# Zeroing a DRAM buffer from the SyncE queue, copied out of DRAM, one head pair earlier

## The chip, the core and the metric

One core of a Trainium2 chip runs the whole kernel. The metric is device time in microseconds (us), from start to end of one execution. Lower is better.

## What is computed

A graph transformer block over N = 1250 nodes with D = 768 features and 20000 edges: a layer norm, then a graph convolution plus polynomial attention over 12 heads, then a switch layer with 8 experts of 195 slots each. Cut to what matters here:

```
xn = _layernorm(x)
A = q @ k.T                              # per head, 1250 x 1250
numerator = 1.0 + A + 0.5 * A * A
attn = numerator / numerator.sum(-1)
mix = (attn @ v) @ w_proj + b_proj
x = x + gnn(xn, edges) + mix
# switch layer on xf = _layernorm(x)
keep = rank < capacity                   # capacity 195 slots for each of 8 experts
buf = zeros(E + 1, capacity, D).at[dest_e, dest_c].set(xf)
o = gelu(buf[:E] @ w1 + b1) @ w2 + b2
out = where(keep, o[routes, dest_c], xf) * prob_max
```

`buf` is what this case is about. A slot that no node is routed to must read as zero, so its DRAM copy, `rows`, is zeroed before the nodes are scattered into it.

## The kernel before

The engines run their own instruction streams and meet at semaphores. Five blocks follow each other.

1. Load, layer norm, transposes and values. VectorE also starts to turn edges into cell indices of `counts`, the 1250 x 1250 table of edge counts in DRAM. GpSimd adds them into that table in indirect transfers, two columns of 128 edges at a time; each pair of columns waits until the pair before has landed.
2. Attention, one head pair after another, j = 0 to 5 (`turn(j, last)` on each engine). A pair is 30 steps: TensorE makes the scores of a step, ScalarE squares them (`Pf`), ScalarE or VectorE rounds them (`Ph`), VectorE makes the rest (`Pl`), TensorE multiplies by `vsb`, the values. Step i's scores need step i-2's squares, since two score buffers alternate. Among the steps of pair j the projections of pair j+1 are made, so that its first step can start at once. GpSimd's edge additions run beside pairs 0 to 5; the last 20 columns are released by VectorE in step 24 of pair 4.
3. `pairs_over`: all engines wait for the end of the pairs. SyncE then also waits for the last edge addition and loads `counts`.
4. Graph convolution, projection, second layer norm, routing.
5. GpSimd scatters the nodes into `rows`; experts; gather and output.

SyncE (SP) issues nearly all transfers, in the order of its code. In pair j it loads the values (`load_v`) and weights (`load_w`), copies each half of the keys to the other 64 partitions (`second_half`: KHB and KLB for the second head, KHA and KLA for the next pair's first head), stores and reloads the inverse denominators (`store_inverse`, `load_inverse`: `invd`, `rden`) and stores the result (`odram`). TensorE's step 0 of the next pair waits for the KHA and KLA copies (`k_twice`), and VectorE's `finish` at step 30 waits for `rden`.

`rows` has 1560 slot rows and 1250 rows for nodes past the capacity, 768 floats each: 2810 x 768 x 4 B = 8.63 MB. ScalarE issues its zeroing in step 4 of the last pair (`CLEAR_AT = 4`), in three transfers out of `strip`, a zeroed SBUF tile of 384 columns. The scatter of block 5 and `pairs_over` wait for it (`r_zero`).

Of the kernel before, what the change touches and what calls it, by code (L numbers as in the profile page):

```python
# [25 lines left out]
F32 = mybir.dt.float32  # L26
F32R = mybir.dt.float32r
BF16 = mybir.dt.bfloat16
# [6 lines left out]
P = 128  # L35
N, D = 1250, 768
T, NT = 125, 10
KT = D // P
HALF = D // 2
# [12 lines left out]
EP = (ET - EARLY) // 5  # L52
# [3 lines left out]
WINDOW = 2  # L56
# [7 lines left out]
CAP = int(1.25 * N / E)  # L64
SLOTS = E * CAP
CAPP = CAP + 1
CTILES = [(0, 105), (105, 90)]
CROWS = 105
STEPS = 30
# [16 lines left out]
def at(start, size):  # L86
    return bass.ds(start, size)
# [3 lines left out]
MOVED = 16 * len(PARTS)  # L91


def move(eng, to, of, landed):

    for p0, n in PARTS:
        eng.dma_start(to[p0:p0 + n], of[p0:p0 + n]).then_inc(landed, 16)  # L97


def build(nc, x, src, dst, gnn_w, gnn_b, w_qkv, b_qkv, w_proj, b_proj, sw, sb_, w1, b1, w2, b2, out,  # L100
          counts, keyd, vdram, odram, rows, x1d, invd):
    ctx = ExitStack()
    with ctx:
        def sem(name):
# [5 lines left out]
        def region(specs):  # L110

            with ExitStack() as inner:
                return [inner.enter_context(nc.sbuf_tensor(*s)) for s in specs]
# [4 lines left out]
        def right(stack, specs):  # L118
# [34 lines left out]
        r_zero = sem("r_zero")  # L153
# [5 lines left out]
        padded = sem("padded")  # L159
        consts, carrier = sem("consts"), sem("carrier")  # L160
# [20 lines left out]

        (K32, kt2, KHA, KLA, MA, gs, Q32, OUN, R32, rden, vsb, tmpo, Pf, Ph, Pl, k1, inv, invr, KHB, KLB, MB, OHL, eqp, kcur, ccur, strip) = region([
            ("K32", [P, N], F32), ("kt2", [P, NT, 2, P], F32R),
            ("KHA", [P, N], F32R), ("KLA", [P, N], F32R), ("MA", [P, N], F32R), ("gs", [P, 3, P], F32),
            ("Q32", [P, N], F32), ("OUN", [P, N], F32), ("R32", [P, N], F32), ("rden", [P, N], F32),
# [1 line left out]
            ("Pf", [T, RING, 2, CW], F32), ("Ph", [T, RING, 2, CW], F32R), ("Pl", [T, RING, 2, CW], F32R),  # L189
            ("k1", [P, 4], F32), ("inv", [T, 2, NT], F32), ("invr", [2 * NT, T], F32),  # L190
            ("KHB", [P, N], F32R), ("KLB", [P, N], F32R), ("MB", [P, N], F32R),
            ("OHL", [P, 2, N], F32R), ("eqp", [P, 2, WINDOW * P], BF16), ("kcur", [P, EP], F32), ("ccur", [P, EP], F32),
            ("strip", [P, HALF], F32)])
        KH, KL, MQ = (KHA, KHB), (KLA, KLB), (MA, MB)
        kbp = kt2[:].rearrange("p t l f -> p (t l) f")
        keys_in, eq_over = sem("keys_in"), sem("eq_over")
# [83 lines left out]
        @block.sync  # L280
        def _(sp):
            for i in range(NT):
                move(sp, xn[:, i, :], x[i * T:(i + 1) * T, :], x_in[i // 2])
                if i == 1:
                    for wc in range(3):
                        sp.dma_start(w_staging(wc), w_parts[0][0][2 * wc * P:2 * (wc + 1) * P, :].rearrange(
                            "(k p) n -> p k n", p=P)).then_inc(w_early[wc], 16)
            sp.wait_ge(keys, 2)
            sp.dma_start(keyd[0:P, :], keyA[:]).then_inc(key_out, 16)
            sp.dma_start(keyd[P:, :], keyB[:]).then_inc(key_out, 16)  # L290
            for s_ in (1, 0):
                sp.dma_start(ws[:, s_], w_qkv[:, s_ * D:s_ * D + P].rearrange("(k p) n -> p k n", p=P)
                             ).then_inc(wqk_in[s_], 16)
            sp.wait_ge(key_out, 32)

            def load_keys(half, slot, c, n):

                sp.dma_start(kb[:, half, slot:slot + n, :], keyd[c:c + n, :].unsqueeze(0).broadcast_to([P, n, P])
                             ).then_inc(kb_in[half], 16)

            load_keys(0, 0, 0, EC)
            sp.wait_ge(w_lo, 3)
            load_keys(1, 0, EC, EC)
            for i in range(NT):
                sp.wait_ge(v_lo, 2 * i + 2)
                move(sp, vdram[:, i, :].rearrange("(j p) f -> p j f", p=T),
                     VS[:, i % 2].bitcast(F32).rearrange("p (j a) l f -> p j (a l f)", a=2), v_store[i % 2])
                if i == FIRST_EDGES + 1:
                    sp.wait_ge(eq_done, 2)
                    load_keys(0, 0, 2 * EC, EC)  # L310
                if i == FIRST_EDGES + 3:
                    sp.wait_ge(eq_done, 4)
                    load_keys(1, 0, 3 * EC, EARLY - 3 * EC)
                    load_keys(1, EARLY - 3 * EC, LONE, 1)
# [319 lines left out]
        def values_over(eng):  # L634

            eng.wait_ge(v_store[0], MOVED * NT // 2)
            eng.wait_ge(v_store[1], MOVED * NT // 2)
            eng.wait_ge(v_mm, 2 * NT)
            eng.wait_ge(idx_ready, EU)
            eng.wait_ge(scattered, CLEARED)  # L640

        PAIR_KEYS_AT = 5
        COMPARE_AT = (6, 7, 7, 8, 10, 10, 11, 12, 13, 14, 15, 15, 16, 17, 17, 18, 20, 20, 21, 22)
        PAIR_TARGETS_AT = 23
        CLEAR_AT = 4

        @block.sync
        def _(sp):
# [16 lines left out]
            def second_half(a, n):  # L665

                own, other = slice(a * HD, (a + 1) * HD), slice((1 - a) * HD, (2 - a) * HD)
                for done, part in ((k_hi[a], KH[a]), (k_lo[a], KL[a])):
                    sp.wait_ge(done, n)
                    sp.dma_start(part[other, :].bitcast(F32), part[own, :].bitcast(F32)).then_inc(k_twice, 16)  # L670
# [14 lines left out]
            def load_inverse(j):  # L685

                sp.wait_ge(inv_out, 16 * j + 16)
                for a in range(2):
                    sp.dma_start(rden[a * HD:(a + 1) * HD, :],
                                 invd[at(j * 2 * NT + a * NT, NT), :].rearrange("i t -> (i t)").unsqueeze(0).broadcast_to([HD, N])  # L690
                                 ).then_inc(rden_in, 16)

            load_pair_keys(0)

            def turn(j, last, keyed):
                sp.wait_ge(oacc_done, 6 * j + FREE)
                load_v(j, 1)
                if not last:
                    sp.wait_ge(wqk_lo, 2 * j + 3)
                    load_w(j + 2, 1)  # L700
                second_half(1, 3 * j + 3)
                if not last:
                    sp.wait_ge(wqk_lo, 2 * j + 4)
                    sp.sem_inc(carrier, 1)
                    load_w(j + 2, 0)
                    store_inverse(j)
                    sp.wait_ge(pv_done, j * STEPS + STEPS // 2)
                    load_v(j + 1, 0)
                    load_inverse(j)
                    second_half(0, 3 * j + 6)  # L710
                    if keyed:
                        load_pair_keys(j + 1)
                else:
                    store_inverse(j)
                    load_inverse(j)
                    sp.wait_ge(g_mm, PAIRS)
                    for wc in (3, 4, 5):
                        load_w3(sp, wc)
                sp.wait_ge(o_fin, 3 * j + 3)
                for l in range(2):  # L720
                    sp.dma_start(odram[at(j * P, P), :, l, :],
                                 OHL[:, l, :].bitcast(F32).rearrange("p (i t) -> p i t", t=T)).then_inc(o_store, 16)
                if not last:
                    sp.wait_ge(o_store, 32 * j + 32)
                    sp.sem_inc(ohl_free, 1)
# [7 lines left out]
        def _(act):  # L733
# [48 lines left out]
            def turn(j, last):  # L782
# [22 lines left out]
                for i in range(END):  # L805
# [8 lines left out]
                        round_weights(i - 1)  # L814
                    if i == OWN_READ_AT:
                        read_kq(j, 5)
                    if last and i == CLEAR_AT:
                        act.wait_ge(padded, 2)
                        act.dma_start(rows[0:SLOTS, :].rearrange("(p s) (h d) -> p (s h) d", p=120, h=2),
                                      strip[0:120, :].unsqueeze(1).broadcast_to([120, 26, HALF])).then_inc(r_zero, 16)  # L820
                        move(act, rows[SLOTS:, :].rearrange("(p s) (h d) -> p (s h) d", p=T, h=2),
                             strip[0:T, :].unsqueeze(1).broadcast_to([T, 2 * NT, HALF]), r_zero)
                    if i in SECOND_AT:
                        hi_part(1, j, SECOND_AT.index(i))
                    if i in LATE_AT:
# [35 lines left out]
        def _(dve):  # L861
# [42 lines left out]
            pair_bias(0)  # L904
            dve.sem_inc(oacc_done, FREE)
            values_over(dve)
            dve.memset(strip[:], 0.0).then_inc(padded, 1)
            before = Chain(dve, pair_order)
            split_w(1, 1)
            for n in range(3):  # L910
# [272 lines left out]
        def pairs_over(eng):  # L1183

            eng.wait_ge(wqk_lo, 2 * PAIRS + 1)
            eng.wait_ge(wqk_in[0], 16 * (PAIRS + 1))
            eng.wait_ge(pv_done, PAIRS * STEPS)
            eng.wait_ge(tmp_done, 6 * PAIRS)
            eng.wait_ge(r_zero, 16 + MOVED)
            eng.wait_ge(o_fin, 3 * PAIRS)  # L1190

        @block.sync
# [307 lines left out]
        @block.gpsimd  # L1500
        def _(pool):
            pool.wait_ge(slot_done, 1)
            pool.wait_ge(xf_done, NT)
            pool.wait_ge(r_zero, 16 + MOVED)
            for i in range(NT):
                pool.indirect_dma_start(out=rows, out_offset=bass.IndirectOffsetOnAxis(ap=slots[:, i:i + 1], axis=0),  # L1506
                                        in_=XF[:, i, :], in_offset=None).then_inc(sent, 16)
# [289 lines left out]
```

## Time and profile before

| what | value |
|---|---|
| median of 3 runs | 1167.61 us (1166.87 to 1172.84) |
| profiled execution, its own time | 1170.61 us |
| its span, first to last instruction | 1168.9 us |
| mean granted TensorE clock | 0.915 |
| busy in the span: TensorE, VectorE, ScalarE, GpSimd | 936.1, 733.1, 459.5, 308.2 us |
| DMA queue 10 (ScalarE's), bytes | 8.80 MB |
| DMA queue 1 (SyncE's), bytes | 128.82 MB |

The profile counts only compute as busy: an engine whose sequencer is held while it issues a transfer shows up as idle, and the issue itself stands in the timeline as ACTq or SPq. All times of rows are from the start of the span, so the profiled execution's own time is 1.7 us more than the span.

### The profile page before, as it was taken

What the parts mean: (1) busy time and instruction counts of PE and PEld (TensorE: products, weight loads), DVE (VectorE), ACT (ScalarE), POOL (GpSimd) and SP (SyncE); (2) the same over time, 40 slices, a digit from 0 to 9 for tenths busy, and PEclk for the clock granted to TensorE, in tenths of its full rate; (3) what the DMA queues carried; (4) which work ended last, traced back from release to release, by engine and by line L of the source; (5) the groups of instructions that cost most, each with busy time, mean ns of one, the idle gap of its engine ahead of it and who ended that gap; (6) DMA issues with size and microseconds to landing.
All of it is one profiled execution on the core that took longest, in us unless ns stands there. A gap on an engine that the chain in (4) does not pass through costs nothing.

```text
span 1168.9 us, 15230 instructions
## 1 busy us (share of the span) xinstructions
PE 936.1 (80%) x5250; PEld 890.3 (76%) x5250; DVE 733.1 (63%) x1397; ACT 459.5 (39%) x678; POOL 308.2 (26%) x201
## 2 busy tenths in 40 slices
PE   3896789989899899899526679699999974199970
PEld 3896788888788789788426579699999974199970
DVE  5776278889878888888425825654454526066633
ACT  2311366666657657566325602111010111166620
POOL 2035465526456445563312000000000002200004
PEclk9898899999999999999859979999999975599995
DMA  9966523543643543732893085462535312879987
GB/s 270 319 167 148 103 23 59 91 77 58 111 71 55 100 70 63 142 51 36 169 210 82 27 155 129 113 159 78 149 88 135 93 57 72 206 232 273 281 221 264
DMA packets 147431, 152.23 MB, mean 130 GB/s; under 512 B 72211, under 2 KB 125546, under 8 KB 146364
## 3 DMA queue, kind: packets, MB, share of 16 engines
q1 hardware_dynamic: 112889, 128.82, 42.4%
q0 software_dynamic: 28432, 14.05, 9.3%
q10 hardware_dynamic: 6067, 8.80, 3.2%
q8 instruction: 26, 0.43, 0.2%
q14 instruction: 17, 0.14, 0.0%
HBM read 97.16 MB, written 46.78 MB: 123 GB/s over the span
## 4 chain that ended last, share of the span: by engine, by line
PE 56%; DVE 15%; issue 9%; ACT 8%; DMA 6%; ACTq 2%; POOL 2%; SPq 1%; DVEq 0%; POOLq 0%
PE ps L1765 13%; PE ps L1767 12%; PE ps L1766 12%; PE ps L1150 6%; PE ps L1134 3%; PE ps L1135 3%; ACT Ph L789 3%; ACT Pf L811 2%; DVE Pl L1008 2%; ACTq L97 2%; DMA rows<-oE 1%; DVE Ph L1006 1%; POOL rows L1506 1%; PE ps L1399 1%; DMA rows<-XF,slots 1%
## 5 line engine op out<-in xcount | busy, mean ns | idle before, releaser
L361 POOL DMA_INDIRECT counts<-countc,idxu x157 | 273.4, 1742 | 321.8 <-DMA counts<-countc,idxu 238.5
L1008 DVE SCALAR_TENSOR_TENSOR Pl<-Pf,Ph 125x832 fp32r<-125x832 f32 (+1 forms) x180 | 184.4, 1026 | 74.1 <-ACT Ph L789 70.3
L811 ACT ACTIVATE Pf<-ps 125x832 f32<-125x832 f32 (+1 forms) x180 | 155.8, 867 | 181.4 <-PE ps L1135 137.8
L1150 PE MATMUL ps<-Ph,vsb 125*128 125x416 f32 (+1 forms) x360 | 132.3, 368 | 9.6 <-DVE Pl L1008 9.5
L1150 PE MATMUL ps<-Pl,vsb 125*128 125x416 f32 (+1 forms) x360 | 128.2, 356 | 0.0
L1506 POOL DMA_INDIRECT rows<-XF,slots x10 | 14.8, 1482 | 361.9 <-DVE slots L1621 359.1
L1134 PE MATMUL ps<-MA,KHA 128*125 128x416 f32 (+1 forms) x180 | 71.1, 395 | 44.2 <-ACT Pf L811 33.8
L1765 PE MATMUL ps<-XH,wqkH 128*128 128x416 f32 (+1 forms) x216 | 81.4, 377 | 19.9 <-DVE R L926 10.2
L1765 PE MATMUL ps<-wH,XH 128*125 128x384 f32 x240 | 85.1, 355 | 9.8 <-DVE OHL L953 5.8
L1150 PEld LDWEIGHTS ps<-Ph,vsb 125*128 125x128 f32 x360 | 69.3, 192 | 19.7 <-DVE Pl L1008 9.3
L1766 PE MATMUL ps<-wL,XH 128*125 128x384 f32 x240 | 83.8, 349 | 0.0
L1767 PE MATMUL ps<-wH,XL 128*125 128x384 f32 x240 | 83.6, 348 | 0.0
L1006 DVE TENSOR_SCALAR Ph<-Pf 125x832 fp32r<-125x832 f32 (+1 forms) x90 | 55.7, 619 | 40.2 <-ACT Pf L811 33.9
L789 ACT ACTIVATE Ph<-Pf 125x832 fp32r<-125x832 f32 (+1 forms) x90 | 79.9, 895 | 0.7
L1766 PE MATMUL ps<-XL,wqkH 128*128 128x416 f32 (+1 forms) x216 | 77.7, 360 | 0.0
L1767 PE MATMUL ps<-XH,wqkL 128*128 128x416 f32 (+1 forms) x216 | 77.7, 360 | 0.0
L1765 PE MATMUL ps<-HH,CH 125*125 125x384 f32 x200 | 69.4, 347 | 7.0 <-DVE CL L1322 7.0
L1134 PE MATMUL ps<-MB,KHB 128*125 128x416 f32 (+1 forms) x180 | 65.7, 365 | 8.5 <-ACT Pf L811 8.5
L1134 PEld LDWEIGHTS ps<-MA,KHA 128*125 128x125 f32 x180 | 34.4, 191 | 49.6 <-ACT Pf L811 40.2
L1150 PEld LDWEIGHTS ps<-Pl,vsb 125*128 125x128 f32 x360 | 69.5, 193 | 0.9
L1767 PE MATMUL ps<-HH,CL 125*125 125x384 f32 x200 | 68.4, 342 | 0.0
L1766 PE MATMUL ps<-HL,CH 125*125 125x384 f32 x200 | 68.4, 342 | 0.0
(236 smaller groups left out, 2176.5 us busy)
## 6 DMA issues: line engine op xcount, KB each, us to landing
Cs<-counts SPq DMA_DIRECT2D x20, 546.9 KB
w1s<-L_ffn_w SPq DMA_DIRECT2D x8, 1152.0 KB, 8.9
w2s<-L_ffn_w SPq DMA_DIRECT2D x8, 1152.0 KB, 6.6
odram<-OHL SPq DMA_DIRECT2D x12, 625.0 KB, 8.5
oS<-odram SPq DMA_DIRECT2D x10, 750.0 KB, 4.8
vdram<-VS SPq DMA_DIRECT2D x10, 672.0 KB
vsb<-vdram SPq DMA_DIRECT2D x12, 560.0 KB
kt<-keyd SPq DMA_DIRECT2D x5, 1280.0 KB, 6.1
```

The costliest lines, as they stand in the source:

```text
L361: pool.indirect_dma_start(out=counts, out_offset=bass.IndirectOffsetOnAxis(ap=idxu[:, c:c + 1], axis=0), in_=countc[:, c:c + 1], in_offset ...
L789: act.activation(Ph[:, i % RING, :, 0:w], Pf[:, i % RING, :, 0:w], ACT.Identity, bias=1.0).then_inc(p_hiA, 1)
L811: act.activation(Pf[:, i % RING, :, 0:w], ps[0:T, 2 * (i % 2):2 * (i % 2) + 2, 0:w], ACT.Square, bias=1.0).then_inc(sq_done, 1)
L1006: dve.tensor_scalar(h, f, 1.0, None, ALU.add).then_inc(p_hiD, 1)
L1008: dve.scalar_tensor_tensor(out=p, in0=f, scalar=1.0, in1=h.bitcast(F32), op0=ALU.add, op1=ALU.subtract).then_inc(p_lo, 1)
L1134: pe.matmul(out_, KH[a][:, kt * T:(kt + 1) * T], q, start=True, stop=False)
L1135: ins = pe.matmul(out_, KL[a][:, kt * T:(kt + 1) * T], q, start=False, stop=True)
L1150: ins = pe.matmul(ps[:, 4 + s % 2, 0:w], vsb[:, 2 * kp + t, a, :], part[:, m % RING, t, 0:w], start=(kp == 0 and t == 0 and part is Ph), s ...
L1506: pool.indirect_dma_start(out=rows, out_offset=bass.IndirectOffsetOnAxis(ap=slots[:, i:i + 1], axis=0), in_=XF[:, i, :], in_offset=None).t ...
L1765: pe.matmul(out, lh, rh, start=(k == 0), stop=False)
L1766: pe.matmul(out, lh, rl, start=False, stop=False)
L1767: ins = pe.matmul(out, ll, rh, start=False, stop=(k == tiles - 1))
```

## The change

The three transfers of ScalarE, the tile `strip` and its memset go. A DRAM tensor `blank` of 1686 floats (6744 B) is written once, early, by a small transfer of SyncE out of the tile `zeros`. In pair 4 (the second-to-last) SyncE then zeroes `rows` in two DRAM to DRAM transfers, each of 16 x 40 runs that all read `blank`: `clear(0)` behind the KLB copy, `clear(1)` between `load_inverse` and the KHA copy. `pairs_over` no longer waits for them; the scatter of block 5 does. Each half is 16 x 40 x 6744 B = 4.32 MB.

```diff
@@ block 1, SyncE
             sp.dma_start(keyd[P:, :], keyB[:]).then_inc(key_out, 16)
+            sp.wait_ge(consts, 1)
+            sp.dma_start(blank.rearrange("(p d) -> p d", p=6), zeros[0:6, 0:BLANK // 6]).then_inc(r_zero, 16)
@@ block 2, SyncE
+            def clear(half):
+
+                n = (SLOTS + N) * D // (32 * BLANK)
+                sp.dma_start(rows.rearrange("r d -> (r d)").rearrange("(a b c) -> a b c", a=16, c=BLANK)[:, half * n:(half + 1) * n],
+                             blank.unsqueeze(0).unsqueeze(0).broadcast_to([16, n, BLANK])).then_inc(r_zero, 16)
+
                 second_half(1, 3 * j + 3)
+                if not last and not keyed:
+                    sp.wait_ge(r_zero, 16)
+                    clear(0)
...
                     load_inverse(j)
+                    if not keyed:
+                        clear(1)
                     second_half(0, 3 * j + 6)
@@ block 2, ScalarE
-                    if last and i == CLEAR_AT:
-                        act.wait_ge(padded, 2)
-                        act.dma_start(rows[0:SLOTS, :].rearrange("(p s) (h d) -> p (s h) d", p=120, h=2),
-                                      strip[0:120, :].unsqueeze(1).broadcast_to([120, 26, HALF])).then_inc(r_zero, 16)
-                        move(act, rows[SLOTS:, :].rearrange("(p s) (h d) -> p (s h) d", p=T, h=2),
-                             strip[0:T, :].unsqueeze(1).broadcast_to([T, 2 * NT, HALF]), r_zero)
@@ block 2, VectorE
-            dve.memset(strip[:], 0.0).then_inc(padded, 1)
@@ pairs_over
-            eng.wait_ge(r_zero, 16 + MOVED)
@@ block 5, GpSimd
-            pool.wait_ge(r_zero, 16 + MOVED)
+            pool.wait_ge(r_zero, 48)
```

ScalarE's queue in the last pair, from step 3's square on. Before:

```order
L747 ACTIVATE Q<-ps,pbias 128x416 [waits qk_mm]
L756 ACTIVATE KHB<-K 64x416 [waits kq_full]
L811 ACTIVATE Pf<-ps 125x836 [waits p_lo,sc_done]
L789 ACTIVATE Ph<-Pf 125x836 [waits pv_done,sq_done]
L819 DMA rows<-strip 3120x1x384 [waits padded]
L97 DMA rows<-strip 2240x1x384
L97 DMA rows<-strip 260x1x384
L811 ACTIVATE Pf<-ps 125x2x416 [waits p_lo,sc_done]
L758 ACTIVATE MA<-Q 64x416 [waits kq_full]
```

Of the change:

```order
L760 ACTIVATE Q<-ps,pbias 128x416 [waits qk_mm]
L769 ACTIVATE KHB<-K 64x416 [waits kq_full]
L824 ACTIVATE Pf<-ps 125x836 [waits p_lo,sc_done]
L802 ACTIVATE Ph<-Pf 125x836 [waits pv_done,sq_done]
L824 ACTIVATE Pf<-ps 125x2x416 [waits p_lo,sc_done]
L771 ACTIVATE MA<-Q 64x416 [waits kq_full]
```

The three transfers between step 4's rounding and step 5's square are gone; the rest stands as it was.

SyncE's queue in pair 4, behind the KLB copy. Before:

```order
L670 DMA KLB<-KLB 64x1250 [waits k_lo1]
L657 DMA ws<-L_mix_w_qkv 128x6x128 [waits wqk_lo]
L683 DMA invd<-invr 20x125 [waits inv_row]
L662 DMA vsb<-vdram 112x10x128 [waits pv_done]
L662 DMA vsb<-vdram 13x10x128
L689 DMA rden<-invd 64x1250 [waits inv_out]
L689 DMA rden<-invd 64x1250
L670 DMA KHA<-KHA 64x1250 [waits k_hi0]
L670 DMA KLA<-KLA 64x1250 [waits k_lo0]
```

Of the change:

```order
L672 DMA KLB<-KLB 64x1250 [waits k_lo1]
L700 DMA rows<-blank 16x40x1686 [waits r_zero]
L659 DMA ws<-L_mix_w_qkv 128x6x128 [waits wqk_lo]
L685 DMA invd<-invr 20x125 [waits inv_row]
L664 DMA vsb<-vdram 112x10x128 [waits pv_done]
L664 DMA vsb<-vdram 13x10x128
L691 DMA rden<-invd 64x1250 [waits inv_out]
L691 DMA rden<-invd 64x1250
L700 DMA rows<-blank 16x40x1686
L672 DMA KHA<-KHA 64x1250 [waits k_hi0]
L672 DMA KLA<-KLA 64x1250 [waits k_lo0]
```

The two halves stand in front of the weights of a later pair and in front of the KHA copy.

## Rows read from the trace of the kernel before

**Rows 1.** The page's first line.

```profile
span 1168.9 us, 15230 instructions
```

**Rows 2.** Timeline of ScalarE in the last pair: start, duration, line, idle before.

```profile
565.93 1.05 ACTq L819 DMA_DIRECT2D rows<-strip  x1
567.02 16.74 ACTq L97 DMA_DIRECT2D rows<-strip  x1
567.03 0.90 ACT L789 ACTIVATE Ph<-Pf 125x836 fp32r<-125x836 f32 x1
583.78 20.94 ACTq L97 DMA_DIRECT2D rows<-strip  x1
604.83 0.86 ACT L811 ACTIVATE Pf<-ps 125x832 f32<-125x832 f32 x1 [36.90 <-issue]
```

**Rows 3.** Timeline of TensorE, same stretch.

```profile
568.58 0.35 PE L1135 MATMUL ps<-MA,KLA 128*125 128x416 f32 x1
...
605.75 0.71 PE L1134 MATMUL ps<-MA,KHA 128*125 128x416 f32 x1 [33.80 <-ACT Pf L811]
...
610.42 0.55 PE L1150 MATMUL ps<-Pl,vsb 125*128 125x416 f32 x1
```

**Rows 4.** Timeline of VectorE, same stretch.

```profile
605.80 0.59 DVE L1006 TENSOR_SCALAR Ph<-Pf 125x832 fp32r<-125x832 f32 x1 [33.86 <-ACT Pf L811]
```

**Rows 5.** Engines' busy times by stretch; then granted clock, DMA share, GB/s.

```profile
488.00:570.00 82.00, 74.45 (x394) 69.50 (x393) 69.69 (x134) 52.37 (x76) 40.07 (x23) 1.00 0.44 69
570.00:675.00 105.00, 51.13 (x233) 44.41 (x232) 51.80 (x68) 40.82 (x52) 17.59 (x10) 0.78 0.51 121
```

**Rows 6.** Chain that ended last, from 560 us on: start, us, what.

```profile
634.04 7.02 DMA wst<-L_gnn_W
...
680.96 10.93 DMA Cs<-counts
```

**Rows 7.** DMA issues: count, KB of each, median us to landing.

```profile
kt<-keyd SPq DMA_DIRECT2D x5, 1280.0 KB, 6.1
counts<-zeros POOLq DMA_DIRECT2D x1, 5468.8 KB, 25.9
...
rows<-strip ACTq DMA_DIRECT2D x1, 4680.0 KB
...
KHA<-KHA SPq DMA_DIRECT2D x6, 312.5 KB, 3.2
```

**Rows 8.** Timeline of SyncE's queue in pair 4.

```profile
494.17 0.50 SPq L670 DMA_DIRECT2D KLB<-KLB  x1
511.64 0.38 SPq L657 DMA_DIRECT2D ws<-L_mix_w_qkv  x1
520.06 0.34 SPq L683 DMA_DIRECT2D invd<-invr  x1
...
522.12 1.16 SPq L689 DMA_DIRECT2D rden<-invd  x2
541.37 0.49 SPq L670 DMA_DIRECT2D KHA<-KHA  x1
548.31 0.48 SPq L670 DMA_DIRECT2D KLA<-KLA  x1
```

**Rows 9.** Timeline of TensorE: the first score of the last pair.

```profile
556.94 0.36 PE L1134 MATMUL ps<-MA,KHA 128*125 128x418 f32 x1
```

**Rows 10.** Timeline of GpSimd: first of a pair of columns, and the last.

```profile
538.16 1.77 POOL L361 DMA_INDIRECT counts<-countc,idxu  x1 [12.54 <-DVE idxu L979]
...
560.90 1.56 POOL L361 DMA_INDIRECT counts<-countc,idxu  x1 [2.05 <-DMA counts<-countc,idxu]
...
614.44 1.56 POOL L361 DMA_INDIRECT counts<-countc,idxu  x1 [9.09 <-DMA counts<-countc,idxu]
...
622.38 2.10 POOL L361 DMA_INDIRECT counts<-countc,idxu  x1 [0.30 <-issue]
```

**Rows 11.** Timeline of SyncE's queue behind the pairs.

```profile
679.39 4.34 SPq L97 DMA_DIRECT2D Cs<-counts  x2
```

More of the change, by code:

```diff
@@ L66 @@
 CAPP = CAP + 1
+BLANK = 1686
 CTILES = [(0, 105), (105, 90)]
@@ L100, in build @@
 def build(nc, x, src, dst, gnn_w, gnn_b, w_qkv, b_qkv, w_proj, b_proj, sw, sb_, w1, b1, w2, b2, out,
-          counts, keyd, vdram, odram, rows, x1d, invd):
+          counts, keyd, vdram, odram, rows, x1d, invd, blank):
     ctx = ExitStack()
@@ L180, in build @@
             ("VS", [T, 2, H, 2, HD], F32R), ("brow", [3 * PAIRS, P], F32)])
-        (K32, kt2, KHA, KLA, MA, gs, Q32, OUN, R32, rden, vsb, tmpo, Pf, Ph, Pl, k1, inv, invr, KHB, KLB, MB, OHL, eqp, kcur, ccur, strip) = region([
+        (K32, kt2, KHA, KLA, MA, gs, Q32, OUN, R32, rden, vsb, tmpo, Pf, Ph, Pl, k1, inv, invr, KHB, KLB, MB, OHL, eqp, kcur, ccur) = region([
             ("K32", [P, N], F32), ("kt2", [P, NT, 2, P], F32R),
@@ L191, in build @@
             ("KHB", [P, N], F32R), ("KLB", [P, N], F32R), ("MB", [P, N], F32R),
-            ("OHL", [P, 2, N], F32R), ("eqp", [P, 2, WINDOW * P], BF16), ("kcur", [P, EP], F32), ("ccur", [P, EP], F32),
-            ("strip", [P, HALF], F32)])
+            ("OHL", [P, 2, N], F32R), ("eqp", [P, 2, WINDOW * P], BF16), ("kcur", [P, EP], F32), ("ccur", [P, EP], F32)])
         KH, KL, MQ = (KHA, KHB), (KLA, KLB), (MA, MB)
@@ L640, in values_over @@
             eng.wait_ge(scattered, CLEARED)
+            eng.wait_ge(r_zero, 16)
         PAIR_KEYS_AT = 5
@@ L644, in build @@
         PAIR_TARGETS_AT = 23
-        CLEAR_AT = 4
         @block.sync
@@ L1794 @@
     invd = nc.dram_tensor("invd", (PAIRS * 2 * NT, T), F32, kind="Internal").ap()
-    build(nc, *args, result, counts, keyd, vdram, odram, rows, x1d, invd)
+    blank = nc.dram_tensor("blank", (BLANK,), F32, kind="Internal").ap()
+    build(nc, *args, result, counts, keyd, vdram, odram, rows, x1d, invd, blank)
     return _run(nc, [arrays], core_ids=[0]).results[0]["out"]
```

## The prediction

> **What bounds the kernel now.** I read the page's chain first. Its two largest entries of one kind outside TensorE's matmuls are transfers issued by ScalarE, so I went to ScalarE's timeline in the last pair. There [rows 2] its sequencer issues the three zeroing transfers. The first is accepted in 1.05 us, the second is held 16.74 us and the third 20.94 us. Behind them in the queue stands the square of step 5, which starts at 604.83 after 36.90 us without compute. Nothing else can go on: TensorE, two score buffers ahead, stands 33.80 us [rows 3], and VectorE, out of squares, 33.86 us [rows 4]. Both name ScalarE's square as what ended the idle time. By stretches [rows 5], the last pair with its end takes 105 us against 82 us for the pair before, with less work in it (TensorE 51 us busy against 74), and at a granted clock of 0.78 against 1.00. So the kernel is bound, in this one place, by ScalarE's sequencer and not by the bytes. The reader is to see that all three compute engines have the same hole.
>
> The hole hides nothing that the end needs. SyncE loads `counts` at 679.39 [rows 11]. The last edge addition is issued at 622.38 [rows 10] and needs a few us to land, so it is over about 50 us before that load.
>
> **The change, part by part.**
>
> *The three transfers leave ScalarE.* Without them, step 5's square waits only for its scores. Their last matmul starts at 568.58 and takes 0.35 us [rows 3], so the square could start at about 569.0 instead of 604.83: ScalarE comes 35.8 us earlier. VectorE's hole begins at 605.80 - 33.86 = 571.94, when that square (0.86 us, over at 569.9) would be done, so VectorE gains its whole 33.9 us. TensorE's hole begins at 605.75 - 33.80 = 571.95 and closes likewise. The least is therefore 33.8 us.
>
> On top of it comes the clock. The matmuls behind the hole take 0.55 us each until 610.42, against 0.35 before it [rows 3]. Between 605.75 and 610.77 TensorE starts some 14 matmuls about 0.35 us apart that it would start 0.19 us apart at full clock: 14 x 0.16 = 2.2 us. VectorE and ScalarE have a share in the pace there, so I count between 0 and 2.2 us of it and take 1. The term is 33.8 + 1 = 34.8, bounds 33.8 and 36.
>
> *What follows the hole* moves forward whole. The next wait for a transfer in the last pair is 7.02 us for the first piece of the next weights [rows 6], issued by SyncE after the inverse is stored. It hangs on step 17 of the same pair, so it moves with the steps and stays as long. The `counts` load moves from 679.39 to about 644.6, and its 10.93 us [rows 6] stay.
>
> *The zeroing becomes part of pair 4.* What must be priced is T, the time of one half of 4.32 MB, DRAM to DRAM. No transfer of that kind is in the trace. Nearest rows [rows 7, 2]: the first zeroing transfer, 4680 KB = 4.79 MB, was drained between 565.93 and 583.78, when the next was let in, which is 268 GB/s and gives T = 16 us. The zeroing of `counts`, 5468.8 KB = 5.60 MB, landed in 25.9 us, which is 216 GB/s and gives T = 20 us. The other side is a transfer that reads first and writes then: 20 us for the writing and, by the key broadcast (1280 KB from one small place in DRAM in 6.1 us, 215 GB/s), 20 us for the reading, so T = 40 us. That is the upper bound. I take T = 20: an engine that reads and writes at the same time is nearer to the `counts` row than to the sum, and the broadcast row shows that reading one small place over and over is not slow.
>
> The Trainium skill, page "DMA: Bandwidth & Descriptors", section "Latency and other measured facts", gives 214 GB/s for copies between HBM tensors, and about half where the rows lie a large power of two apart. Here the 16 destination rows lie 80 x 6744 B = 539,520 B apart, which is none. By that rate T would be 20.2 us, and the forecast would be the same. The same page, section "Bandwidth", puts the HBM limit of a core at about 358 GB/s; if reading and writing both draw on it, 8.63 MB for each half would make T = 24 us, and the sum would be 2 us worse by the formula below. No run here shows either yet.
>
> *Who waits for the two halves.* `clear(0)` is issued right behind KLB at 494.7 [rows 8]. It starts to move at about 498, since the value load, the weights and the two key copies are ahead of it. It ends at 498 + T = 518. The next things on the queue are weights of a pair that doesn't exist (511.64, nobody waits) and the inverse (520.06): with T under 21 both are untouched. `clear(1)` goes out at 523.3, behind the value load and the two `rden` transfers. Together they are about as many bytes as the key broadcast of 6.1 us [rows 7], so it starts to move at about 529. It ends at 529 + T = 549. Behind it stand KHA (issued 541.37) and KLA (548.31), 3.2 us each to land when alone [rows 7, 8]. Before, KLA was there at 551.6; now both land at about 552 to 553. TensorE's first score of the last pair, which waits for them, is at 556.94 [rows 9]. So at T = 20 there are some 4 us to spare and the cost is nothing. The cover is thin. Once T is over 21, `clear(0)` pushes the inverse, that pushes `clear(1)`, and both land on KHA: `clear(1)` ends at 508 + 2T, the copies land 3 us later, and the stall is 511 + 2T - 557 = **2T - 46 us**, zero at T = 23.
>
> *If SyncE is held at its issues* as ScalarE was, KHA is issued only when `clear(1)` is drained (549) and lands at 552.5, and KLA at about 556. That is still in time, by under 1 us; I add nothing.
>
> *The edge additions.* They share the 16 DMA engines. A pair of columns took (560.90 - 538.16) / 4 = 5.7 us undisturbed and (614.44 - 560.90) / 4 = 13.4 us beside the zeroing, so the zeroing cost them 4 x 7.7 = 31 us [rows 10]. Now they lose this in pair 4. The last ten pairs of columns are released at 538.16 after GpSimd idled 12.54 us, which absorbs that much. Undisturbed they would end at 538 + 10 x 5.7 + 2 = 597. If they stand still for both halves, they end at 597 + 40 - 12.5 = 625. The `counts` load is at 644.6: hidden, with 20 us to spare.
>
> *The rest.* `blank` costs SyncE one more small issue (the comparable one at 520.06 takes 0.34 us [rows 8]) in front of weights that are needed much later. The memset of `strip` stood alone, and `pairs_over` found `r_zero` long done. All of it: nothing.
>
> **The sum.** 33.8 + 1 - 0 = 34.8 us. The profiled execution's own time, 1170.6 (1.7 us over its span [rows 1]), becomes 1135.8. It was 3.0 us above the median of the three runs shown; from that median, 1167.6 - 34.8 = 1132.8. I forecast 1133.
>
> **Rivals.**
>
> 1. *The halves are hidden, as above*: 1131 to 1136. For it: T = 20 by the nearest row. Against: 3 us of T decide. Chance 0.68.
> 2. *The key copies come late.* T between 24 and 38. For it: every byte is now read from and written to DRAM, the additions take their share, and the cover is thin. Against: the rows of 16 and 20 us. At T = 26 the stall is 6 us and the time 1139; at T = 30 it is 14 and 1147; at T = 36 it is 26 and 1159. Chance 0.22, most of it (0.14) below 1150.
> 3. *Slower than before.* The same mechanism at a low rate: it decides at 2T - 46 > 34.8, so T > 40.4 us or under 107 GB/s, half of the `counts` row. At T = 45 the stall is 44 us and the time 1177. For it: no DRAM to DRAM row at all, and 640 runs out of one place of 6.7 KB. Against: the key broadcast reads such a place at 215 GB/s. Chance 0.04.
> 4. *The edge additions end too late.* Long runs of 6744 B in the queues of the same engines could hold the additions more than the runs of 1536 B did. They decide when they lose more than 60 us (597 - 12.5 + 60 = 644.6). A loss of 70 us gives 1143. Against: standing still for both halves is only 40. Chance 0.04.
> 5. *Nothing gained*: the hole was not the issue of these transfers but the busy DMA engines. Then it would go to another place of pair 4 or 5, 1167. Against: no row of the three holes names a transfer. Chance 0.02.
>
> **Range and chances.** 1129 to 1149: the first case with 2 to 4 us for what measurement and clock make of it, and the second up to T = 31. This leaves out some 1.5 in 10. What a measurement of this kernel can tell from no change is about 0.5%, or 6 us: faster holds everything below 1162, that is cases 1, 2 and 4, 0.94 in all; same 0.03; slower 0.03.
>
> **What would show it.** Right: no ACTq transfer in the last pair; no idle time above some 3 us on the three engines around its step 5; granted clock 1.00 there; two rows of 0.4 to 1 us for `rows<-blank` on SyncE, and a DMA share near 1 for 20 us behind each; the first score of the last pair within 1 us of 557; the edge additions over by 625. Wrong: a wait of step 0 of the last pair on KHA or KLA, whose length gives T; `finish` of pair 4 waiting for `rden`; SyncE held at an issue behind `clear`; a `counts` load released by an edge addition.

## The result and the profile after

| | before | changed |
|---|---|---|
| median | 1169.7 us (4 runs, 1166.87 to 1172.84) | 1135.14 us (4 runs, 1130.86 to 1136.78) |
| ratio | | 0.9698, 95% interval 0.9672 to 0.9725 |
| profiled execution, span | 1168.9 us | 1132.4 us |
| granted TensorE clock | 0.915 | 0.928 |

The ratio is 35.3 us of 1169.7. The forecast was 1133 and a gain of 34.8.

The timeline of ScalarE in the last pair, which answers to [rows 2]:

```profile
565.30 0.87 ACT L824 ACTIVATE Pf<-ps 125x836 f32<-125x836 f32 x1
566.19 0.90 ACT L802 ACTIVATE Ph<-Pf 125x836 fp32r<-125x836 f32 x1
568.18 0.87 ACT L824 ACTIVATE Pf<-ps 125x832 f32<-125x832 f32 x1 [1.09 <-PE ps L1141]
```

The hole of 36.90 us is 1.09 us, and what ends it is the score matmul, as between any two steps. The timeline of SyncE's queue in pair 4, which answers to [rows 8]:

```profile
493.51 0.50 SPq L672 DMA_DIRECT2D KLB<-KLB  x1
494.06 0.64 SPq L700 DMA_DIRECT2D rows<-blank  x1
511.04 0.38 SPq L659 DMA_DIRECT2D ws<-L_mix_w_qkv  x1
519.46 0.34 SPq L685 DMA_DIRECT2D invd<-invr  x1
519.85 1.62 SPq L664 DMA_DIRECT2D vsb<-vdram  x2
521.51 1.17 SPq L691 DMA_DIRECT2D rden<-invd  x2
522.73 0.63 SPq L700 DMA_DIRECT2D rows<-blank  x1
540.48 0.50 SPq L672 DMA_DIRECT2D KHA<-KHA  x1
547.42 0.48 SPq L672 DMA_DIRECT2D KLA<-KLA  x1
```

The two issues take 0.64 and 0.63 us, and everything behind them is issued within 1 us of where it was before. How long they run is read from short windows of the same trace (engines' busy times, then granted clock, DMA share, GB/s):

```profile
494.00:514.00 20.00, 19.89 (x112) 18.96 (x111) 16.08 (x34) 12.99 (x18) 3.51 (x3) 1.00 1.05 264
514.00:516.00 2.00, 2.00 (x12) 1.76 (x10) 1.75 (x5) 0.58 (x1) 1.70 (x2) 1.00 0.38 110
516.00:520.00 4.00, 3.19 (x16) 2.68 (x16) 3.81 (x13) 3.14 (x7) 2.26 (x2) 1.00 0.22 0
...
528.00:544.00 16.00, 16.00 (x89) 15.50 (x88) 12.97 (x26) 11.70 (x19) 4.04 (x2) 1.00 1.03 264
544.00:546.00 2.00, 2.00 (x12) 1.97 (x11) 2.00 (x4) 1.98 (x3) 1.38 (x1) 1.00 0.03 8
```

The DMA engines are full, then nearly empty: the first half is over by 515, the second by 544 to 545. With KLB landing at 498.5 and the `rden` loads at about 528, a half takes T = 16 to 17 us, at 264 GB/s in all traffic of the window. TensorE meanwhile is busy in 19.89 of 20 us at full clock. The first score of the last pair, the first load of `counts` and the last edge addition, three timelines (TensorE, SyncE, GpSimd) that answer to [rows 9, 11, 10]:

```profile
556.10 0.36 PE L1140 MATMUL ps<-MA,KHA 128*125 128x418 f32 x1
```

```profile
642.51 18.01 SPq L98 DMA_DIRECT2D Cs<-counts  x6
```

```profile
608.14 2.12 POOL L363 DMA_INDIRECT counts<-countc,idxu  x1 [0.30 <-issue]
```

The first score comes 0.8 us earlier than before, the `counts` load 36.9 us earlier. So 36.0 us were won inside the last pair and nothing was paid in pair 4. That load itself takes 12.48 us in the chain against 10.93 before [rows 6], so its landing moved by 34.8 us. The end of the span moved by 36.5 us; where the last 1.7 us come from was not looked into.

### The profile page after: what moved, and what is told of

It is laid out like the page before. It is cut to its first block, busy times and chain, and to the rows that moved or that the text cites. A ratio compares the mean times of both kernels' runs of the same rounds, so it can differ in the third digit from the quotient of the medians.

```text
span 1132.4 us, 15230 instructions
## 1 busy us (share of the span) xinstructions
PE 931.7 (82%) x5250; PEld 886.2 (78%) x5250; DVE 733.0 (65%) x1396; ACT 459.4 (41%) x678; POOL 308.5 (27%) x201
## 3 DMA queue, kind: packets, MB, share of 16 engines
HBM read 105.79 MB, written 46.78 MB: 135 GB/s over the span
## 4 chain that ended last, share of the span: by engine, by line
PE 57%; DVE 15%; ACT 9%; issue 8%; DMA 7%; POOL 2%; SPq 1%; DVEq 0%; ACTq 0%; POOLq 0%
PE ps L1770 14%; PE ps L1772 13%; PE ps L1771 13%; PE ps L1156 6%; PE ps L1140 3%; ACT Ph L802 3%; PE ps L1141 3%; ACT Pf L824 2%; DVE Pl L1014 2%; DVE Ph L1012 1%; DMA rows<-oE 1%; POOL rows L1511 1%; DMA Cs<-counts 1%; PE ps L1404 1%; PE ps L1116 1%
## 5 line engine op out<-in xcount | busy, mean ns | idle before, releaser
L1141 PE MATMUL ps<-MB,KLB 128*125 128x416 f32 (+1 forms) x180 | 64.2, 357 | 0.0
L1141 PE MATMUL ps<-MA,KLA 128*125 128x416 f32 (+1 forms) x180 | 64.1, 356 | 0.0
```

Of the source, the lines that this page charges most:

```text
L1141: ins = pe.matmul(out_, KL[a][:, kt * T:(kt + 1) * T], q, start=False, stop=True)
```

## The experiments

All ratios are to the kernel before, timed on the same chip in the same rounds.

### 1. The copies stay in the last pair, on ScalarE

```diff
 # changed kernel, both clear() calls of SyncE taken out, and on ScalarE:
+                    if last and i == 4:
+                        for half in range(2):
+                            act.dma_start(rows...[:, half * n:(half + 1) * n],
+                                          blank...broadcast_to([16, n, BLANK])).then_inc(r_zero, 16)
```

> The two DRAM to DRAM halves (16 x 40 runs of 6744 B each) are issued by ScalarE in step 4 of the last pair, where the three strip transfers stood in the kernel before; SyncE issues none. Theory A (the hole was ScalarE's sequencer held at its issues, and it is held when the transfers in front of it are made of many runs, 208 runs per DMA engine in the first strip transfer): 40 runs per engine are taken at once, two issues of about 0.6 us, hole under 2 us, time 1134 to 1138. Theory B (what cost the time was 8.6 MB on the DMA engines at that place, whoever issues them): hole of about 30 us again, time 1160 to 1170. Theory C (any second large transfer is held until the first has drained, however few its runs): one hold of about 16 us on ScalarE, time 1149 to 1153.

Measured: 1154.04 us, ratio 0.9873 (0.9854 to 0.9891). None of the three. ScalarE's timeline has the two issues and no hole:

```profile
565.01 0.69 ACTq L828 DMA_DIRECT2D rows<-blank  x1
...
565.73 0.65 ACTq L828 DMA_DIRECT2D rows<-blank  x1
566.11 0.90 ACT L797 ACTIVATE Ph<-Pf 125x836 fp32r<-125x836 f32 x1
568.05 0.87 ACT L819 ACTIVATE Pf<-ps 125x832 f32<-125x832 f32 x1 [1.04 <-PE ps L1141]
```

So A is right on ScalarE, and C falls. But the chain that ended last, in this kernel, has a new link (start, us, what):

```profile
572.24 2.91 SPq L664
575.20 3.87 SPq L672
579.11 29.01 DMA KLB<-KLB
608.16 0.71 PE ps L1140
```

The KLB copy, issued by SyncE on its own queue, lands 29.0 us later, where before and after the change its median is some 5 us. TensorE, due at step 15, stands 21.6 us for it. 8.6 MB at this place cost the time a second way: the zeroing fills the DMA engines in front of a copy that is wanted 7 us after its issue (579.1, wanted at 586.5). In the kernel before this was hidden behind the hole, since the KHB and KLB copies were issued only at 607.5 and 611.1, when the zeroing was nearly over. SyncE is held too, 3.87 us at KHB and 3.00 at KLB, though its own queue has only the value loads and KHB in front of them. Theory A alone would have given 1135; the 19 us above it (20 by the ratios) hang on the place.

### 2. The same with short runs

```diff
-BLANK = 1686
+BLANK = 281          # 240 runs of 1124 B per engine and half in place of 40 of 6744 B
```

> As the kernel with both copies on ScalarE in the last pair, but out of runs of 1124 B: 240 per engine and half in place of 40. Theory A (number of runs): the second half is held until the first has drained, 16 to 20 us of hole, time 1150 to 1156. Theory D (what held ScalarE was the SBUF source or the partition count, not the runs): no hole, 1134 to 1138.

Measured: 1236.39 us, ratio 1.0576 (1.0555 to 1.0597). ScalarE's timeline:

```profile
566.15 0.69 ACTq L828 DMA_DIRECT2D rows<-blank  x1
...
566.87 46.18 ACTq L828 DMA_DIRECT2D rows<-blank  x1
...
613.15 0.86 ACT L819 ACTIVATE Pf<-ps 125x832 f32<-125x832 f32 x1 [45.01 <-issue]
```

The second issue is held 46.18 us against 0.65 us with 40 runs per engine, from DRAM both times. So a sequencer is held without any SBUF source (D falls); with the same bytes, it is the number of runs that decides. The time missed both theories, because these runs move at 67 to 68 GB/s in the windows between 566 and 600, a quarter of the rate of the long ones. With the runs in front draining so slowly, a hold longer than the 16 to 20 us of A fits A's mechanism. Experiment 7 asks why they are slow.

### 3. One strip transfer left on ScalarE

```diff
 # kernel before, on ScalarE
-                        move(act, rows[SLOTS:, :]..., strip...[T, 2 * NT, HALF], r_zero)
 # and on SyncE in pair 4, behind KLB
+                    sp.dma_start(rows[SLOTS:, :]...(16 x 100 runs), blank...).then_inc(r_zero, 16)
```

> The kernel before with only the first of the three strip transfers (4.79 MB, 208 runs per engine) on ScalarE in step 4 of the last pair; the 3.84 MB of node rows are copied DRAM to DRAM by SyncE in pair 4 behind the KLB copy. Theory A: this transfer was accepted in 1.05 us before and is so again, nothing on ScalarE stands behind it in its queue, hole about 1 to 2 us, time 1135 to 1139. Theory B (bytes at that place): 4.8 of 8.6 MB are left, so a bit more than half of the hole, 18 us, time about 1152.

Measured: 1138.31 us, ratio 0.9748 (0.9731 to 0.9764), as A says. The issue takes 1.06 us again and ScalarE's next square waits 1.04 us. What is left over the changed kernel, 3 us in the medians and 6 by the ratios, is again the copy: KLB lands after 16.5 us and TensorE waits 7.6 us for it.

### 4. Two strip transfers on ScalarE

```diff
 # kernel before; only the third transfer (13 partitions, 0.40 MB) goes to SyncE in pair 4
-                        move(act, rows[SLOTS:, :]..., strip...)
+                        act.dma_start(rows[SLOTS:SLOTS + 1120, :]..., strip[0:112, :]...).then_inc(r_zero, 16)
```

> The kernel before with the first two strip transfers on ScalarE in step 4 of the last pair and only the third, the small one over 13 partitions, taken out (0.40 MB, copied DRAM to DRAM by SyncE in pair 4). Theory A (an issue is held by what is queued in front of it): the second is held about 17 us as before, the third's 21 us are gone; the hole is 17 us, and then the rest of the zeroing delays the KLB copy, which must be there at step 15, by some us more: time 1150 to 1156. Rival (the third transfer's hold was free, since the key copy would have waited as long anyway): 1160 to 1167.

Measured: 1149.94 us, ratio 0.9829 (0.9806 to 0.9851), the lower edge of A. The second issue is held 16.50 us, and the copy follows:

```profile
583.31 0.71 PE L1141 MATMUL ps<-MA,KHA 128*125 128x416 f32 x1 [12.61 <-ACT Pf L818]
605.30 0.46 PE L1141 MATMUL ps<-MB,KHB 128*125 128x418 f32 x1 [3.72 <-DMA KLB<-KLB]
```

Two rows of TensorE share the loss, 12.6 us for ScalarE and 3.7 us for KLB. Taking out the smallest transfer, 5% of the bytes, wins 20 us of the 35.

### 5. The strips of before, at the places of the change

```diff
 # kernel before, ScalarE's three transfers taken out; on SyncE in pair 4:
+                    sp.dma_start(rows[0:SLOTS, :]..., strip[0:120, :]...)      # behind KLB
+                        move(sp, rows[SLOTS:, :]..., strip[0:T, :]..., r_zero)  # behind load_inverse
```

> The three strip transfers of the kernel before, out of SBUF, issued by SyncE in pair 4 at the two places of the changed kernel (first behind the KLB copy, second and third behind the inverse's reload). Theory P (place and issuing engine are what matters, not the DRAM source): the third holds SyncE until the second has drained, about 20 us, so KHA goes out at about 545 and both key copies land by 552, before the first score: time 1134 to 1139. Theory S (runs of 1536 B out of SBUF hold SyncE longer than the cover): the first score waits on the KHA or KLA copy, 1140 to 1155.

Measured: 1131.23 us, ratio 0.9674 (0.9656 to 0.9692). Theory P, though the time lies 3 us below the range that I gave for it. SyncE's timeline:

```profile
495.39 1.00 SPq L704 DMA_DIRECT2D rows<-strip  x1
...
527.08 1.17 SPq L689 DMA_DIRECT2D rden<-invd  x2
528.29 6.78 SPq L97 DMA_DIRECT2D rows<-strip  x2
541.89 0.52 SPq L670 DMA_DIRECT2D KHA<-KHA  x1
```

SyncE is held 6.78 us, not the 20 I expected, and would have stood idle in that time anyhow. KHA goes out in time. The interval overlaps that of the changed kernel, so the DRAM source, one half of what the change does, is worth nothing that could be measured. Queue and place are all of it.

The windows of this trace also show how fast the strips move, all traffic counted:

```profile
500.00:520.00 20.00, 19.47 (x111) 18.51 (x110) 17.80 (x37) 12.98 (x20) 6.03 (x4) 1.00 0.94 191
532.00:540.00 8.00, 8.00 (x45) 7.58 (x44) 6.70 (x16) 6.20 (x12) 3.11 (x2) 1.00 1.06 352
```

The first strip moves at 191 GB/s, the second and third at about 352, though the runs of all three are 1536 B long. Why they differ no run takes apart.

### 6. How thick the cover is: one place, and twice the bytes

```diff
 # both late: changed kernel
-                if not last and not keyed:
-                    sp.wait_ge(r_zero, 16)
-                    clear(0)
...
+                        clear(0)
                         clear(1)
```

> The changed kernel with both halves issued where the second stood, between the inverse's reload and the KHA copy. With the 16 us per half that the changed kernel's trace shows, they are drained at about 528 + 32 = 560 and the KHA and KLA copies land at about 563, against a first score due at 556: stall of about 7 us, time 1139 to 1144. Rival (the cover is wider than I thought, so one place would do): 1134 to 1137.

```diff
 # twice: a copy of the same size into a spare tensor behind each half
                     clear(0)
+                    clear(0, spare)
...
                         clear(1)
+                        clear(1, spare)
```

> The changed kernel with each half followed by a second copy of the same size into a spare DRAM tensor that nobody reads, so that each place carries 8.63 MB. From the changed kernel's trace a half took 16 to 17 us, so T is now 32 to 34 us. My formula for the stall of the last pair's first score, 2T - 46, gives 18 to 22 us: time 1153 to 1157, the first score waiting on the KHA or KLA copy. Rival (the copies to the key halves are not behind the zeroing, since the DMA engines take turns among transfers): stall under 5 us, 1135 to 1140.

Measured: 1146.7 us, ratio 0.9798 (0.9772 to 0.9824), and 1152.23 us, ratio 0.986 (0.984 to 0.9879). TensorE's first score of the last pair, both late:

```profile
567.74 0.72 PE L1138 MATMUL ps<-MA,KHA 128*125 128x418 f32 x1 [8.37 <-DMA KLA<-KLA]
```

and twice:

```profile
576.17 0.71 PE L1142 MATMUL ps<-MA,KHA 128*125 128x418 f32 x1 [18.83 <-DMA KLA<-KLA]
```

The stalls are 8.4 us (7 expected) and 18.8 us (18 to 22 expected): the key copies do wait behind the zeroing, by about what the formula says. The doubled kernel's time is 1 us under the range that I gave. The time with both halves late is 2.7 us above its range. Its trace shows two things that I had not counted: the granted clock of TensorE is 0.50 in 560 to 570, and pair 4 itself is 3.1 us late by the storing of the inverse (522.58 against 519.46 in the changed kernel), at a granted clock of 0.91 in 494 to 512. Which of them it is was not tried.

### 7. Why short runs are slow

```diff
 # own places: runs of 1124 B, each engine reads its own
-blank.unsqueeze(0).unsqueeze(0).broadcast_to([16, n, BLANK])
+blank[:, 0:BLANK].unsqueeze(1).broadcast_to([16, n, BLANK])    # blank is (16, 1250)
```

> The changed kernel with runs of 1124 B (240 per engine and half), as in the kernel with short runs on ScalarE, which moved only 60 to 70 GB/s; but each of the 16 DMA engines reads a run of its own, 5000 B from the next, and not all the same 1124 B. Theory F (the low rate came of all engines reading one small place): the rate is back near 270 GB/s, a half takes 16 to 18 us, time 1133 to 1138. Theory G (a DRAM to DRAM run costs a fixed time, so short runs are slow wherever they are read): again 60 to 70 GB/s, a half takes about 63 us, stall 2T - 46 = 80 us, time 1205 to 1225, slower than the kernel before.

```diff
 # short runs: changed kernel
-BLANK = 1686
+BLANK = 281
```

> The changed kernel with runs of 1124 B that all read the same 1124 B (240 per engine and half), SyncE issuing both halves in pair 4 as in the changed kernel. On ScalarE such runs moved 60 to 70 GB/s. T is then about 60 us and the first score of the last pair stands about 2T - 49 = 70 us (the constant as the doubled and the own-places kernel show it, where the key copies landed with the end of the zeroing and not 3 us behind it): time 1195 to 1215, slower than the kernel before. If the low rate belonged only to ScalarE's queue or to the last pair: 1134 to 1150.

Measured: 1146.18 us, ratio 0.9792 (0.9765 to 0.9818), and 1231.09 us, ratio 1.0526 (1.0507 to 1.0546). The windows, own places and short runs:

```profile
494.00:512.00 18.00, 18.00 (x103) 17.25 (x102) 14.70 (x31) 11.12 (x16) 3.11 (x2) 1.00 1.14 177
...
530.00:540.00 10.00, 10.00 (x55) 9.57 (x54) 8.76 (x19) 8.06 (x13) 3.97 (x2) 1.00 1.04 194
540.00:550.00 10.00, 10.00 (x56) 9.68 (x54) 7.27 (x13) 8.43 (x14) 2.76 (x2) 1.00 1.18 144
```

```profile
512.00:540.00 28.00, 26.71 (x139) 25.02 (x138) 25.77 (x56) 18.87 (x29) 3.91 (x2) 1.00 1.02 58
540.00:570.00 30.00, 12.06 (x65) 11.10 (x63) 9.57 (x15) 9.32 (x15) 3.11 (x2) 0.76 1.02 60
```

Neither F nor G alone. The same 1124 B for all engines: 58 to 60 GB/s. Sixteen places, same length: 144 to 194 GB/s, where the rows of 177 and 194 hold the KLB copy and the `rden` loads as well; from 500 to 512, without them, it is 150. Long runs from one place of 6744 B: 264 GB/s. Reading one very small place from all engines is worth a factor of about 2.5; what is left to the long runs is a factor of 1.8, from length or from still few places, which was not taken apart.

Experiment 3 has a point in between, 100 runs of 2400 B per engine that all read the same 2400 B:

```profile
504.00:520.00 16.00, 15.06 (x82) 13.87 (x81) 14.54 (x35) 10.10 (x17) 3.87 (x2) 1.00 0.89 126
```

As an estimate from these rates, with 16 engines at work, one run takes 0.30 us when all read the same 1124 B (59 GB/s) and 0.30 us when all read the same 2400 B (126 GB/s), but 0.12 us when each reads 1124 B of its own (150 GB/s). By these two points a small shared place costs a time per run and not per byte. At 6744 B it is 0.41 us per run.

The short-run kernel is rival 3 of the prediction come true. TensorE's rows:

```profile
582.27 2.50 PE L1085 MATMUL ps<-kt 125*128 125x256 f32 x10 [28.88 <-DVE kt L898]
654.12 0.71 PE L1140 MATMUL ps<-MA,KHA 128*125 128x418 f32 x1 [69.34 <-DMA KLA<-KLA]
```

4.32 MB at 60 GB/s are T = 72 us, and 2T - 49 (below) gives 95; the two waits are 98 us. It comes in two pieces: VectorE's `finish` waits 27.75 us for `rden`, then the first score for KLA. I had given 1195 to 1215 with T = 60. SyncE is held on the way, 27.05, 17.32 and 17.19 us at its next three issues behind the first half and 42.88 us at KHA behind the second.

### 8. A version that is faster than both

In the changed kernel ScalarE waits 8.05 us in the last pair for the first of the next weights, and VectorE 10.6 us behind it. Both loads write where only K32 and the transposed keys lay; by the KLB copy's wait and the one for `g_mm` both are used up.

```diff
                 else:
+                    sp.wait_ge(g_mm, PAIRS)
+                    for wc in (3, 4):
+                        load_w3(sp, wc)
                     store_inverse(j)
                     load_inverse(j)
-                    sp.wait_ge(g_mm, PAIRS)
-                    for wc in (3, 4, 5):
-                        load_w3(sp, wc)
+                    load_w3(sp, 5)
```

> The changed kernel with the first two loads of the next weights issued in the last pair ahead of the storing of the inverse, right behind the KLB copy, and the third behind the reload of the inverse. In the changed kernel's trace ScalarE waits about 7 us for the first of them in step 18 and VectorE 10 us behind it. Theory: that wait goes, 5 to 8 us, time 1127 to 1131. Rival (the wait only moves to the third load or to the end of the pair): within 2 us of the changed kernel, 1133 to 1137.

> As the kernel with the early weight loads, and the two small loads of the router's bias and weights, whose issues take 1.7 and 1.2 us in front of the counts load after the pairs, are moved into the last pair too. Theory: the counts load is issued 3 us earlier, time 1124 to 1129. Rival (something else ends last there): as the kernel with the early weight loads alone.

Measured: 1125.49 us, ratio 0.9625 (0.96 to 0.965), and with the two small loads moved as well 1125.41 us, ratio 0.9631 (0.9609 to 0.9653). The early loads win 0.7% over the changed kernel by the ratios, and the time lies 1.5 us under the range that I gave. The small loads win nothing that could be measured. The chain of the first kernel and that of the second show why:

```profile
634.45 2.32 SPq L98
636.81 10.84 DMA Cs<-counts
647.67 2.47 DVE csum L1307
```

```profile
633.25 1.18 SPq L98
634.47 13.64 DMA Cs<-counts
648.14 2.47 DVE csum L1307
```

The load is issued earlier and lands as late, 13.64 us against 10.84. The wait went from the issue into the transfer.

## Why the prediction was right, point by point

**The three transfers leave ScalarE: 34.8 us, bounds 33.8 and 36.** Measured 36.0 inside the last pair (36.9 less the 0.8 us with which it started earlier), the upper bound. The 33.8 of the hole is confirmed by the row of 1.09 us. The rest is the clock, and the same 16 matmuls in both traces show its size. Before, they run from 605.75 [rows 3] to the next group:

```profile
611.20 0.86 PE L1102 MATMUL ps<-Q,gs 128*128 128x416 f32 x2
```

In the changed kernel they run from 570.98 to 574.05:

```profile
570.98 0.35 PE L1140 MATMUL ps<-MA,KHA 128*125 128x416 f32 x1
...
574.05 0.86 PE L1108 MATMUL ps<-Q,gs 128*128 128x416 f32 x2
```

That is 5.45 us, most of it at a granted clock of 0.50, against 3.07 at 1.00: 2.4 us. I took 1 because VectorE and ScalarE might set the pace there; they do not.

**What follows the hole.** The wait for the first of the next weights is 6.68 us in the chain against 7.02, as said. The transfer of `counts` did not stay at 10.93 us but took 12.48, and the span won 1.7 us behind it. The sum had neither; that they nearly cancel is luck.

**T = 20 us.** 16 to 17, at the lower bound. But the row behind that bound was misread. I took the first strip transfer for drained when the second had been let in, at 583.78, which gave 268 GB/s. ScalarE's queue (q10) had moved less by then, in 566 to 584:

```profile
q10 hardware_dynamic: 2036, 3.13, 75.2%
```

That is 3.13 MB of 4.79, or 174 GB/s beside 41 GB/s of other traffic, which would have put T at 20 to 25. So no row that the prediction drew on had the rate of 264 GB/s that the copies reach, and that the bound of 16 us was met is luck. The error was on the safe side, and T = 20 was right in what it decided, that the halves are hidden.

By the Trainium skill's figure of 214 GB/s for copies between HBM tensors (page "DMA: Bandwidth & Descriptors", section "Latency and other measured facts") T would have been, as an estimate, 20.2; this trace has 264 GB/s in all traffic of the window, so the measurement decides against it. The limit of about 358 GB/s (same page, section "Bandwidth"), read as shared by reading and writing, would have given 24 us, and this trace goes against that reading too. The profile counts 105.79 MB read from HBM after against 97.16 before, 8.63 more, and 46.78 MB written in both, so by its count the halves were read at about 264 GB/s and written at about 264 at once.

**The stall 2T - 46.** Right in form, 3 us too large. In the doubled kernel the DMA engines move 251 to 256 GB/s, so 8.63 MB take T = 34 us; 2T - 46 gives 22 and the stall is 18.8. That fits key copies that land with the end of the zeroing and not 3 us behind it: 2T - 49, zero at T = 24 to 25. With own places the stall is 7.1 us, but the rate there varies too much (144 to 194 GB/s) to tell the two apart. In the changed kernel the copies land at 545.3 and 550.6, with 5.5 us to spare before 556.1.

**"If SyncE is held at its issues."** It was not, at 40 runs per engine.

**The edge additions: over by 625.** Their last issue is at 608.14. They lost less than a standstill, and GpSimd no longer waited for new columns in pair 4, where it had idled 12.54 us before [rows 10]: that time absorbed the rest, as said.

**What bounds the kernel: "ScalarE's sequencer and not the bytes".** This is the step that was incomplete, though it did not touch the number. The hole was the sequencer's, as shown by experiments 1, 3, 4 and 5. But experiment 1 shows that the same bytes at the same place, with ScalarE not held, still cost 21.6 us through the KLB copy. The forecast came out because this change moved the bytes as well. Had it only freed ScalarE, my sum would have been some 19 us too good. In the profile before, the row that would have warned is the KLB copy's own issue time: it stood behind the hole, and the question to ask was what it would meet once the hole was gone.

**The broadcast row as evidence that one small place is read fast.** True for its 10,240 B (1280 KB for 128 partitions) and for 6744 B, false for 2400 and 1124 B.

## What to carry to other kernels

A compute engine that issues a transfer can be held there, by the runs already in front of it; read the issue rows of its queue, and move the issue to a queue with idle time, before asking how many bytes there are. An issue that is let in does not show that what stood in front of it has landed; ask the bytes of the queue. When a hole closes, look at every transfer that used to be issued behind it and ask what it will now run into: here freeing the engine alone would have kept 14 of 35 us. A bulk transfer belongs where the next transfer that somebody waits for is further away than its own length, and its source should be large enough that not all DMA engines read the same kilobyte.

## What the runs showed of the hardware

- **Who is held at an issue.** Often it is the small transfer over 13 partitions, and about until what is in front of it has drained. In the doubled kernel the value load over 112 partitions is issued in 1.33 us and the one over 13 right behind it in 10.23; with own places 0.67 and 5.68 us; in the kernel before, the third strip transfer takes 20.94 us, and when it is let in 8.0 of the 8.2 MB in front of it have moved. The second, over 112 partitions, is let in with 3.1 of 4.8 MB moved. The Trainium skill says (page "DMA: Bandwidth & Descriptors", section "Why a DMA increments its semaphore by 16 and not by 1") that a transfer runs on the largest number of engines up to 16 that divides the outer dimension of both its sides, so on 13 here; whether that is what holds it, no run here shows. The number of runs in the queue counts too: the strip transfer over 112 partitions was held 16.5 us behind 208 runs per engine (3120 runs, on 15 engines by the same rule), and the KHA copy over 64 partitions 9.82 us behind 240, but 0.50 us behind 80 long ones. Traffic of the other queue counts as well: with both copies on ScalarE, SyncE is held 3.87 us at a copy of 64 partitions. The two strips at SyncE, held 6.78 us together, fit no plain rule of full drainage. The rule stays open; that the hold depends on the runs and not on the bytes is shown by 0.65 against 46.18 us.
- **A read of one small place.** 58 to 60 GB/s for 1124 B read by all 16 engines, 126 GB/s for 2400 B, 264 GB/s for 6744 B; about 150 GB/s for 16 places of 1124 B.
- **DRAM to DRAM with long runs against SBUF to DRAM.** 264 GB/s in runs of 6744 B; the strips, in runs of 1536 B, 191 GB/s for the first and 352 for the other two (experiment 5). Source, run length and partition count differ at once, so none of it can be put down to the source.
